# Eleven tables instead of nine by one-hot matmul, two at a time, in a DLRM tower on one core

## The chip, the cores and the metric

One Trainium2 chip, one of its cores. The metric is the time of one execution on the device in microseconds (us); lower is better. Engines: TensorE (PE; its weight loads are PEld), VectorE (DVE), ScalarE (ACT), GpSimd (POOL) and SyncE (SP), which here only issues DMAs.

## The reference

For 512 samples, 26 embedding rows of 128 numbers are looked up, one from each of 26 tables (1000, 1250, 12500 or 125000 rows). With the sample's bottom vector they make 27 features. All 351 dot products of two different features, and the bottom vector, go through three layers. All is float32.

```python
e = jnp.stack([tbl_0[ids[:, 0]], ..., tbl_25[ids[:, 25]]], axis=1)
all_emb = jnp.concatenate([bottom_output[:, None, :], e], axis=1)
gram = jnp.einsum('bfd,bgd->bfg', all_emb, all_emb)
z = gram[:, _TRIU_I, _TRIU_J]
h = jnp.concatenate([z, r_bottom_output], axis=1)
h = jnp.maximum(h @ W_top1 + b_top1, 0.0)
h = jnp.maximum(h @ W_top2 + b_top2, 0.0)
y = h @ W_top3
```

## The kernel before, in words

The samples are four tiles of 128. Features sit in 27 slots: slot 0 is the bottom vector, slots 1 to 9 are the tables that are looked up by matmul (`LOOKED_UP`, nine tables of 1000 rows), slots 10 to 26 the 17 others, gathered row by row.

**Lookup.** A table of 1000 rows lies in SBUF as 125 partitions of 8 rows (`VK`). For each k of the 8, a one-hot matrix of 125 x 512 says which sample wants row 8p + k. TensorE multiplies the table's k-th 125 x 128 slice by it, for all 512 samples at once, and sums over k in PSUM. Precision comes from two terms: the table's value rounded to fp32r (`tab_hi`, cast by ScalarE at line 473) and the rest (`tab_lo`, subtracted by VectorE at line 332); the matmuls are at lines 721 and 725. The one-hots come from `hot`, the table's 512 ids on every partition as int32, minus the partition's first row (line 383). VectorE compares with k (line 388) for 6 or 7 of the 8, ScalarE does the others with a square and a relu (lines 479, 483). A ring of 14 one-hots, a ring of 3 tables and ids, and two split copies of tables tie the engines together by semaphores: the ring places are given back by `s_look`, which TensorE's low matmuls increment. ScalarE copies the found rows from PSUM to `embT` (line 545), the feature matrix with the dimension on partitions, the samples and then the 27 features on the free axis.

**Gathers.** GpSimd issues one indirect DMA of 128 rows for every tile and gathered table (line 313, 68 in all), tile by tile; `emb` has two tiles, so tile 2 waits until the same bank of tile 0 has been transposed. A bank is up to four slots (`BANKS`, five a tile, the last with one slot). TensorE transposes a bank into PSUM (line 612), VectorE (line 329) and ScalarE (line 461) copy banks to `embT` in turn.

**The order after the lookups** is written out by hand, one list for each engine. `gram(t, half)` makes the 27 x 27 products of 64 samples (line 624, two halves a tile). `copy_stage` (line 219) and `copy_products` (line 230) bring them from PSUM to SBUF, split between VectorE and ScalarE; three DMAs move the staged columns to their partitions in `prod` (line 243). `high_products` (line 499) and `low_products` (line 332) split `prod`; layer 1 multiplies the bottom vector's part and the products' part with the split weights (lines 632, 633, 640) into `pH1`; relu (line 522), transpose of h1 (line 676), its split (lines 529, 332), layer 2 (with the bias rows, lines 687, 688) and layer 3 on VectorE (line 372) follow. The weights come in seven chunks of 512 columns into the places of the last tables (line 270) and are split by ScalarE (line 489) and VectorE. Tiles 2 and 3 copy their grams in halves. Before layer 1 of tile 3 TensorE does eight matmuls whose result nobody reads (`stay_busy(WAIT_MOVES)`, line 709).

The DMA queues: SP issues the ids as indices, the tables, `hot` for tables 1 to 8, bottom, b2, w3, the weights and the moves, in program order; ScalarE's queue has `hot` for table 0 alone, GpSimd's the gathers.

Of the kernel before, what the change touches and what calls it, by code (L numbers as in the profile page):

```python
# [21 lines left out]
B = 512  # L22
D = 128
# [13 lines left out]
WAIT_MOVES = 8  # L37
# [4 lines left out]
LOOKED_UP = [3, 4, 5, 7, 8, 10, 20, 24, 25]  # L42
LOOKED = len(LOOKED_UP)
VOCAB = 1000
VP = 125
VP_MAIN = VP // 16 * 16
VK = VOCAB // VP
FIRST_CHUNKS = 2
RING = 3
HOT_RING = 14  # L50
CHUNKS = KTILES + 1 + 2
CHUNK_RING = 2 * RING
# [9 lines left out]
def dve_tiles(i):  # L62

    return VK - 1 - i % 2


def act_tiles_before(i):
    return i * VK - sum(dve_tiles(j) for j in range(i))

# [5 lines left out]
def tower(nc, bottom, ids, hot_ids, tables, w1, w2, b2, w3, out):  # L75
    fp32, fp32r, i32 = mybir.dt.float32, mybir.dt.float32r, mybir.dt.int32
# [3 lines left out]
    with ctx:  # L80
# [10 lines left out]
        hot = sb("hot", [128, RING, B], i32)  # L91

        row0 = sb("row0", [VP, 1], i32)
        row0f = sb("row0f", [VP, 1])
        minus_k = sb("minus_k", [VP, 2])
        tab = sb("tab", [128, RING, VK, D])
        tab_hi = sb("tab_hi", [VP, 2, VK, D], fp32r)
        tab_lo = sb("tab_lo", [VP, 2, VK, D], fp32r)
        square = sb("square", [VP, B])
        onehot = sb("onehot", [VP, HOT_RING, B], fp32r)  # L100
# [9 lines left out]
        w_hi = sb("w_hi", [128, CHUNKS, N1], fp32r)  # L110
        w_lo = sb("w_lo", [128, CHUNKS, N1], fp32r)
# [19 lines left out]
        s_hotids = [sem(f"s_hotids{i}") for i in range(LOOKED)]  # L131
# [9 lines left out]
        s_row0f = sem("s_row0f")  # L141
        s_rel = sem("s_rel")
# [37 lines left out]
        w1_hi, w1_lo = w_hi[:, 0:KTILES + 1, :], w_lo[:, 0:KTILES + 1, :]  # L180
        w2_hi, w2_lo = (w[:, KTILES + 1:, :].rearrange("p c (k n) -> p (c k) n", n=N2) for w in (w_hi, w_lo))
# [10 lines left out]
        def hot_rows(i, k):  # L192
            return onehot[:, (i * VK + k) % HOT_RING, :]

        def wait_hot_free(engine, i, k):

            if i * VK + k >= HOT_RING:
                engine.wait_ge(s_look, i * VK + k - HOT_RING + 1)

        def chunk(c):  # L200

            table = (LOOKED + (c % CHUNK_RING) // 2) % RING
            return tab[:, table, VK // 2 * (c % 2):VK // 2 * (c % 2 + 1), :].rearrange("p k d -> p (k d)")

        def even(t, i):
            return (t * len(BANKS) + i) % 2 == 0
# [40 lines left out]
        def _(sp):  # L247
            def load_table(i, p0, p1, k0, k1, loaded):

                sp.dma_start(tab[p0:p1, i % RING, k0:k1, :], tables[LOOKED_UP[i]].rearrange(  # L250
                    "(p k) d -> p k d", k=VK)[p0:p1, k0:k1, :]).then_inc(loaded, 16)

            def load_lookup(i):
                if i >= RING:
                    sp.wait_ge(s_look, (i - RING + 1) * VK)
                sp.dma_start(hot[:, i % RING, :], hot_ids[i:i + 1, :].broadcast_to([128, B])).then_inc(s_hotids[i], 16)
                load_table(i, 0, VP_MAIN, 0, VK, s_tab[i])
                load_table(i, VP_MAIN, VP, 0, VK, s_tab[i])

            def load_weights(c):  # L260
                if c < CHUNK_RING:
                    sp.wait_ge(s_look, (LOOKED - RING + c // 2 + 1) * VK)
                else:
                    sp.wait_ge(s_wlo, c - CHUNK_RING + 1)
                if c <= KTILES:
                    dst, src = chunk(c), w1[:, c, :]
                else:
                    dst = chunk(c).rearrange("p (k n) -> p k n", n=N2)
                    src = w2.rearrange("(k p) n -> p k n", p=128)[:, 2 * (c - KTILES - 1):2 * (c - KTILES), :]
                sp.dma_start(dst, src).then_inc(s_w[c], 16)  # L270
# [3 lines left out]
            load_table(0, 0, VP_MAIN, 0, VK // 2, s_tab[0])  # L274
            load_table(0, VP_MAIN, VP, 0, VK, s_tab[0])
            load_table(0, 0, VP_MAIN, VK // 2, VK, s_tab0_rest)
            sp.dma_start(bot[:, :, :], bottom.rearrange("(p t) d -> p t d", t=TILES)).then_inc(s_bot, 16)
            load_lookup(1)
            load_lookup(2)
            sp.dma_start(b2s[:, :], b2.unsqueeze(0)).then_inc(s_small, 16)  # L280
            sp.dma_start(w3s[:, :], w3.rearrange("n o -> o n").broadcast_to([128, N2])).then_inc(s_small, 16)
            for i in range(RING, LOOKED):
                load_lookup(i)
# [15 lines left out]
        def _(pool):  # L299
            nc.gpsimd.iota(row0[:, :], [[0, 1]], base=0, channel_multiplier=VK).then_inc(s_row0, 1)  # L300
# [534 lines left out]
```

## Time and profile before

| | us |
|---|---|
| median of 3 runs | 126.18 (125.71 to 126.25) |
| the profiled execution | 124.48 |
| its span, first to last instruction | 122.6 |

Busy in that span: TensorE 90.8, weight loads 73.3, VectorE 77.2, ScalarE 78.4, GpSimd 73.7. The granted clock of TensorE is 0.916 on average. In the rows, the start of an instruction or of a run of equal ones is in us from the span's start; "x8" is a count; what stands after the bar or in brackets is the engine's idle time before it and what ended it. Some matmul records can be missing from a trace.

### The profile page before, as it was taken

The numbers are of one execution on the slowest core, as the hardware profiler recorded it, in microseconds if no ns is written. First come the engines' busy times: TensorE is split into PE (matmuls) and PEld (weight loads), VectorE is DVE, ScalarE is ACT, GpSimd is POOL, SyncE is SP. The second block draws the span as 40 slices with busy tenths as digits, with TensorE's granted clock in tenths as the row PEclk, the third lists the DMA queues.
The fourth block names the chain that finished last, engine by engine and source line by source line (L and its number), as shares of the span: only waits on it lengthen the run. The fifth ranks groups of instructions, "written<-read, shape, count | busy, mean of one in ns | idle before, by whom it ended". The sixth has DMA issues, their size and how long they took to land.

```text
span 122.6 us, 3473 instructions
## 1 busy us (share of the span) xinstructions
PE 90.8 (74%) x1395; PEld 73.3 (60%) x1395; DVE 77.2 (63%) x182; ACT 78.4 (64%) x146; POOL 73.7 (60%) x76
## 2 busy tenths in 40 slices
PE   0005999989989969975318865498998993499992
PEld 0004788858866648854207654396786873488971
DVE  1009999999999996449683158904896328933021
ACT  6214799999999899785405849830899246950130
POOL 3877887788888878888877778787777100100000
PEclk9999999999999999999965799855999999855999
DMA  2789948988988993581222213121221100000000
GB/s 78 211 259 254 241 132 247 235 220 203 222 225 210 242 261 60 204 282 44 68 56 63 55 43 76 43 68 49 52 67 47 43 0 8 8 17 0 0 0 1
DMA packets 7000, 14.08 MB, mean 115 GB/s; under 512 B 2026, under 2 KB 2675, under 8 KB 6984
## 3 DMA queue, kind: packets, MB, share of 16 engines
q1 hardware_dynamic: 4632, 9.11, 27.5%
q0 software_dynamic: 2208, 4.48, 14.8%
q10 hardware_dynamic: 144, 0.26, 0.9%
q8 instruction: 11, 0.18, 0.6%
q14 instruction: 5, 0.04, 0.1%
HBM read 13.71 MB, written 0.00 MB: 112 GB/s over the span
## 4 chain that ended last, share of the span: by engine, by line
POOL 38%; PE 30%; issue 17%; ACT 9%; DMA 3%; DVE 1%; DVEq 0%
POOL emb L313 38%; PE pG L624 7%; PE pH L632 5%; ACT prod L230 5%; PE pH L633 4%; PE pH L640 4%; PE pT L612 2%; PE pG L676 2%; DMA emb<-tbl,idx 2%; PE pT L709 2%; ACT stage L219 2%; DMA idx<-ids 1%; PE pH L687 1%; ACT w_hi L489 1%; PE pH L688 1%
## 5 line engine op out<-in xcount | busy, mean ns | idle before, releaser
L313 POOL DMA_INDIRECT emb<-tbl,idx x68 | 72.4, 1064 | 21.7 <-issue 20.1
L721 PE MATMUL pG<-onehot,tab_hi 125*128 125x512 f32 x72 | 21.0, 431 | 13.0 <-DVE onehot L388 10.6
L721 PEld LDWEIGHTS pG<-onehot,tab_hi 125*128 125x128 f32 x72 | 14.0, 202 | 17.4 <-issue 14.9
L388 DVE TENSOR_SCALAR onehot<-hot 125x512 fp32r<-125x512 int32 x59 | 22.1, 441 | 0.3
L725 PE MATMUL pG<-onehot,tab_lo 125*128 125x512 f32 x72 | 18.0, 391 | 0.0
L624 PE MATMUL pG<-embT 128*26 128x26 f32 x1024 | 13.5, 200 | 5.2 <-issue 4.0
L624 PEld LDWEIGHTS pG<-embT 128*26 128x26 f32 x1024 | 11.6, 112 | 8.5 <-issue 6.2
L612 PE MATMUL pT<-ident,emb 128*128 128x128 f32 x68 | 11.0, 289 | 6.1 <-DMA emb<-tbl,idx 4.7
L725 PEld LDWEIGHTS pG<-onehot,tab_lo 125*128 125x128 f32 x72 | 13.7, 190 | 3.0
L230 ACT COPY prod<-pG 14x64 f32<-14x64 f32 (+7 forms) x48 | 14.7, 306 | 0.6
L230 DVE COPY prod<-pG 14x64 f32<-14x64 f32 (+7 forms) x48 | 14.5, 303 | 0.7
L473 ACT CAST tab_hi<-tab 125x1024 fp32r<-125x1024 f32 (+1 forms) x10 | 9.8, 981 | 5.2 <-DMA tab<-tbl 4.4
L612 PEld LDWEIGHTS pT<-ident,emb 128*128 128x128 f32 x68 | 8.3, 146 | 7.7 <-DMA emb<-tbl,idx 5.0
L219 ACT COPY stage<-pG 10x160 f32<-10x160 f32 (+1 forms) x12 | 6.4, 535 | 9.8 <-PE pG L624 9.6
L329 DVE COPY embT<-pT 128x512 f32<-128x512 f32 (+1 forms) x10 | 6.3, 631 | 9.0 <-PE pT L612 9.0
L479 ACT ACTIVATE square<-hot,minus_k 125x512 f32<-125x512 int32 x13 | 9.4, 725 | 3.5 <-DVE hot L383 3.4
L461 ACT COPY embT<-pT 128x512 f32<-128x512 f32 (+1 forms) x10 | 6.4, 636 | 8.0 <-PE pT L612 8.0
L332 DVE TENSOR_TENSOR tab_lo<-tab,tab_hi 125x1024 fp32r<-125x1024 f32 x9 | 11.0, 1218 | 0.8 <-ACT tab_hi L473 0.7
L545 ACT COPY embT<-pG 128x512 f32<-128x512 f32 x9 | 10.9, 1207 | 0.8 <-PE pG L725 0.8
L383 DVE TENSOR_SCALAR hot<-hot,row0f 125x512 int32<-125x512 int32 x9 | 4.6, 507 | 8.3 <-DMA hot<-hot_ids 8.3
L483 ACT ACTIVATE onehot<-square,ones 125x512 fp32r<-125x512 f32 x13 | 9.4, 724 | 0.4
L219 DVE COPY stage<-pG 10x160 f32<-10x160 f32 (+1 forms) x12 | 6.4, 533 | 3.6 <-PE pG L624 3.4
(69 smaller groups left out, 114.0 us busy)
## 6 DMA issues: line engine op xcount, KB each, us to landing
tab<-tbl SPq DMA_DIRECT2D x8, 448.0 KB
hot<-hot_ids SPq DMA_DIRECT2D x8, 256.0 KB, 4.5
tab<-w SPq DMA_DIRECT2D x7, 256.0 KB, 3.4
emb<-tbl,idx POOLq DMA_INDIRECT x68, 4.4
tab<-tbl SPq DMA_DIRECT2D x9, 52.0 KB
tab<-tbl SPq DMA_DIRECT2D x2, 224.0 KB, 3.8
bot<-bottom SPq DMA_DIRECT2D x1, 256.0 KB, 6.6
hot<-hot_ids ACTq DMA_DIRECT2D x1, 256.0 KB, 6.7
```

What stands on the lines that cost most here:

```text
L219: last = copy(stage[:, :, 64 * halves[0] + s:64 * (halves[-1] + 1):4].rearrange("p k (b i) -> p b i k", i=BANK_GROUPS), gram_blocks(t)[32 ...
L230: last = copy(prod[32 * j:32 * j + rows, :, 64 * halves[0] + s:64 * (halves[-1] + 1):4].rearrange("p k (b i) -> p b i k", i=BANK_GROUPS), ...
L313: nc.gpsimd.indirect_dma_start(out=emb[:, t % 2, g - LOOKED - 1, :], out_offset=None, in_=tables[f], in_offset=bass.IndirectOffsetOnAxis(a ...
L332: return nc.vector.tensor_tensor(lo, whole, hi, ALU.subtract)
L388: nc.vector.tensor_scalar(hot_rows(i, k), hot[0:VP, i % RING, :], float(k), None, ALU.is_equal).then_inc(s_hotv, 1)
L473: nc.scalar.copy(tab_hi[:, i % 2, k:k + step, :], tab[0:VP, i % RING, k:k + step, :]).then_inc(s_tabhi, 1)
L479: nc.scalar.activation(square[:, :], hot[0:VP, i % RING, :], ACT.Square, bias=minus_k[:, k - VK + 2:k - VK + 3]).then_inc(s_sq, 1)
L545: nc.scalar.copy(embT[:, :, :, 1 + i], pG[i % 2][:, 0, :].rearrange("d (t p) -> d t p", p=128)).then_inc(s_lookc, 1)
L612: last = nc.tensor.transpose(bank(t, i)[:, m, :], emb[:, t % 2, g - LOOKED - 1, :], ident[:, :])
L624: last = nc.tensor.matmul(gram_blocks(t)[32 * s:32 * s + ROWS, half, i, :], embT[:, t, p, 0:ROWS], embT[:, t, p, 1:FEATURES], start=True, ...
L721: nc.tensor.matmul(pG[i % 2][:, 0, :], tab_hi[:, i % 2, k, :], hot_rows(i, k), start=(k == 0), stop=False)
L725: nc.tensor.matmul(pG[i % 2][:, 0, :], tab_lo[:, i % 2, k, :], hot_rows(i, k), start=False, stop=(k == VK - 1)).then_inc(s_look, 1)
```

## The change

- `LOOKED_UP` gets two more tables, 2 and 9, of 1250 rows (10 rows a partition). Eleven tables are looked up, 15 are gathered (60 gathers). Banks are four a tile: 4, 4, 4 and 3 slots.
- Table 0 is looked up alone, the others in five pairs (`PAIRS`). A step is one k of a pair: one one-hot instruction for 2 x 512 columns, then four matmuls. The ring holds 8 steps. All one-hots are VectorE's. The comparison is with the row number, which is read per partition, so the subtraction at line 383 goes.
- The ids lie in SBUF for all eleven tables at once, as the low 16 bits (`hot` is int16), loaded in three parts: table 0 by ScalarE's queue, tables 1 and 2, and tables 3 to 10, by SP's, ahead of bottom.
- Tables have four places; high and low parts too, and the split weights lie in the same places afterwards. A table's load waits for the subtraction of the table before it in its place.
- One copy brings both found tables of a pair to `embT`.
- The banks of tiles 0 and 1 are transposed between the pairs (`BANKS_AFTER_PAIR`) and copied by ScalarE alone. In tiles 2 and 3 both engines copy banks in turn, as before.
- In the last tiles the order changes, and `stay_busy` goes.

The diff's core:

```diff
-LOOKED_UP = [3, 4, 5, 7, 8, 10, 20, 24, 25]
+LOOKED_UP = [3, 4, 5, 7, 8, 10, 20, 24, 25, 2, 9]
+VK = [8, 8, 8, 8, 8, 8, 8, 8, 8, 10, 10]
+HOT_RING = 8
+SLOTS = 4
+PAIRS = [range(0, 1)] + [range(i, i + 2) for i in range(1, LOOKED, 2)]
+HOT_PARTS = [range(0, 1), range(1, 3), range(3, LOOKED)]
+BANKS_AFTER_PAIR = {1: [(0, 0)], 2: [(0, 1)], 3: [(0, 2), (0, 3)], 4: [(1, 0), (1, 1)], 5: [(1, 2), (1, 3)]}
...
+        hot = sb("hot", [128, LOOKED, B], i16)
+        tab = sb("tab", [128, SLOTS, VK_MAX, D])
+        high = sb("high", [128, SLOTS, VK_MAX, D], fp32r)
+        low = sb("low", [128, SLOTS, VK_MAX, D], fp32r)
+        onehot = sb("onehot", [VP, HOT_RING, 2, B], fp32r)
...
 SP:
+            def load_whole_table(i):
+                if slot_before(i) >= 0:
+                    sp.wait_ge(s_tablo, slot_before(i) + 1)
...
             load_table(0, 0, VP_MAIN, VK[0] // 2, VK[0], s_tab0_rest)
+            load_hot_ids(1)
+            load_whole_table(1)
+            load_whole_table(2)
+            load_hot_ids(2)
             sp.dma_start(bot[:, :, :], ...)
             b2s, w3s
+            for i in range(3, LOOKED):
+                load_whole_table(i)
...
 VectorE:
+            for n, pair in enumerate(PAIRS):
+                dve.wait_ge(s_hotids[min(n, 2)], 16)
+                following = PAIRS[n + 1] if n + 1 < len(PAIRS) else []
+                for k in range(STEPS[n]):
+                    step = STEPS_BEFORE[n] + k
+                    if step >= HOT_RING:
+                        dve.wait_ge(s_look, step - HOT_RING + 1)
+                    nc.vector.tensor_scalar(hot_rows(n, k), hot[0:VP, pair[0]:pair[-1] + 1, :],
+                                            rowf[VK[pair[0]]][:, k:k + 1], None, ALU.is_equal).then_inc(s_hot, 1)
+                    if n > 0 and k == 3 and following:
+                        low_table(following[0])
+                if n == 0:
+                    low_table(0)
+                    low_table(following[0])
+                if following:
+                    low_table(following[-1])
+            low_weights(0, 4)
...
             copy_stage(0)
             copy_bank(2, 0)
             copy_products(0)
+            low_weights(4, KTILES + 1)
             low_products(0)
...
 ScalarE:
+            for i in range(3):
+                high_table(i)
+            for n in range(len(PAIRS)):
+                copy_found(n)
+                if n + 2 < len(PAIRS):
+                    for i in PAIRS[n + 2]:
+                        high_table(i)
...
+                for t, i in BANKS_AFTER_PAIR.get(n, []):
+                    copy_bank(t, i)
+                if n == len(PAIRS) - 2:
+                    high_weights(0, 4)
+            high_weights(4, CHUNKS)
...
             copy_stage(3, [0])
             copy_products(3, [0])
+            high_h1(2)
             copy_stage(3, [1])
             copy_products(3, [1])
             high_products(3)
...
 TensorE:
+            for n in range(1, len(PAIRS)):
+                pair = PAIRS[n]
+                if n >= 2:
+                    pe.wait_ge(s_lookc, n - 1)
+                pe.wait_ge(s_tablo, pair[-1] + 1)
+                for k in range(STEPS[n]):
+                    pe.wait_ge(s_hot, STEPS_BEFORE[n] + k + 1)
+                    for i in pair:
+                        look(n, i, k, high, k == 0, False)
+                    for i in pair:
+                        last = look(n, i, k, low, False, k == STEPS[n] - 1)
+                    last.then_inc(s_look, 1)
...
+                for t, i in BANKS_AFTER_PAIR[n]:
+                    transpose_bank(t, i)
...
+            pe.wait_ge(s_lookc, len(PAIRS))
             gram(0, 0)
-            transpose_bank(1, 2)
-            transpose_bank(1, 3)
-            transpose_bank(1, 4)
             gram(0, 1)
             transpose_bank(2, 0)
-            transpose_bank(2, 1)
             gram(1, 0)
             layer1_bottom(0)
             gram(1, 1)
+            transpose_bank(2, 1)
             layer1_products(0)
             transpose_bank(2, 2)
             transpose_h1(0)
+            layer2(0)
             transpose_bank(2, 3)
-            layer2(0)
-            transpose_bank(2, 4)
...
             layer2(1)
+            layer1_bottom(2)
+            whole, = h1_parts(2)
+            layer1_high(2, whole, range(0, 2))
             transpose_bank(3, 2)
-            layer1_bottom(2)
-            layer1_products(2)
+            layer1_high(2, whole, range(2, 3))
             transpose_bank(3, 3)
-            transpose_bank(3, 4)
+            layer1_high(2, whole, range(3, 4))
+            layer1_low(2, whole)
+            gram(3, 0)
             transpose_h1(2)
-            gram(3, 0)
             gram(3, 1)
             layer2(2)
             layer1_bottom(3)
-            stay_busy(WAIT_MOVES)
```

## Rows read from the trace of the kernel before

**Rows 1.** Page, part 5: the gathers on GpSimd.
```profile
L313 POOL DMA_INDIRECT emb<-tbl,idx x68 | 72.4, 1064 | 21.7 <-issue 20.1
```

**Rows 2.** Timeline: the joints between the phases (start, length, engine, operation).
```profile
49.44 1.98 PE L725 MATMUL pG<-onehot,tab_lo 125*128 125x512 f32 x8
51.26 1.04 PE L612 MATMUL pT<-ident,emb 128*128 128x128 f32 x8
...
52.69 1.71 PE L624 MATMUL pG<-embT 128*26 128x26 f32 x128 [0.39 <-ACT embT L545]
...
64.41 1.12 PE L612 MATMUL pT<-ident,emb 128*128 128x128 f32 x4 [2.64 <-DMA emb<-tbl,idx]
...
83.86 2.07 PE L624 MATMUL pG<-embT 128*26 128x26 f32 x128 [0.50 <-DVE embT L329]
```

**Rows 3.** Groups by line and form (busy us, mean ns of one, idle before).
```profile
L388 DVE TENSOR_SCALAR onehot<-hot 125x512 fp32r<-125x512 int32 x59 | 22.1, 441 | 0.3
...
L725 PE MATMUL pG<-onehot,tab_lo 125*128 125x512 f32 x72 | 18.0, 391 | 0.0
...
L332 DVE TENSOR_TENSOR tab_lo<-tab,tab_hi 125x1024 fp32r<-125x1024 f32 x9 | 11.0, 1218 | 0.8 <-ACT tab_hi L473 0.7
L545 ACT COPY embT<-pG 128x512 f32<-128x512 f32 x9 | 10.9, 1207 | 0.8 <-PE pG L725 0.8
...
L473 ACT CAST tab_hi<-tab 125x1024 fp32r<-125x1024 f32 x8 | 8.6, 1072 | 2.5 <-DMA tab<-tbl 1.7 <-PE pG L725 0.8
...
L461 ACT COPY embT<-pT 128x512 f32<-128x512 f32 x8 | 5.5, 689 | 7.0 <-PE pT L612 7.0
...
L332 DVE TENSOR_TENSOR w_lo<-tab,w_hi 128x512 fp32r<-128x512 f32 x7 | 4.5, 684 | 2.1 <-ACT w_hi L489 2.1
```

**Rows 4.** Timeline of DVE: the first one-hots.
```profile
9.96 2.58 DVE L388 TENSOR_SCALAR onehot<-hot 125x512 fp32r<-125x512 int32 x7
```

**Rows 5.** Page, part 6: DMA issues (count, KB each, us to landing).
```profile
tab<-tbl SPq DMA_DIRECT2D x8, 448.0 KB
hot<-hot_ids SPq DMA_DIRECT2D x8, 256.0 KB, 4.5
...
tab<-tbl SPq DMA_DIRECT2D x9, 52.0 KB
```

**Rows 6.** Windows from the start (last columns: clock, DMA share, GB/s); ScalarE's wait for table 1.
```profile
0.00:9.00 9.00, 0.00 (x0) 0.00 (x0) 0.34 (x4) 3.13 (x4) 5.71 (x12) 1.00 0.63 182
9.00:14.00 5.00, 3.37 (x8) 2.76 (x9) 4.52 (x10) 2.33 (x3) 3.80 (x4) 1.00 1.04 254
...
13.12 1.04 ACT L473 CAST tab_hi<-tab 125x1024 fp32r<-125x1024 f32 x1 [1.68 <-DMA tab<-tbl]
```

**Rows 7.** Windows with low granted clock (PE, PEld, DVE, ACT, POOL busy; clock, DMA).
```profile
64.40:68.50 4.10, 3.38 (x133) 2.87 (x134) 1.09 (x3) 2.86 (x7) 3.16 (x4) 0.50 0.20 52
...
106.40:113.80 7.40, 6.24 (x25) 5.57 (x25) 3.05 (x11) 2.64 (x9) 0.56 (x1) 0.54 0.03 8
```

**Rows 8.** Stage and product copies of tile 0 in the timeline; the relu's group.
```profile
59.15 1.42 ACT L219 COPY stage<-pG 10x320 f32<-10x320 f32 x2 [1.17 <-PE pG L624]
...
62.41 3.10 DVE L230 COPY prod<-pG 14x128 f32<-14x128 f32 x8
...
L522 ACT ACTIVATE h<-pH 128x256 f32<-128x256 f32 x7 | 2.4, 382 | 9.2 <-PE pH L640 9.2
```

**Rows 9.** Timeline of tile 3: the last high products, and TensorE around the fillers.
```profile
108.90 0.62 ACT L499 CAST prod_hi<-prod 128x512 fp32r<-128x512 f32 x1 [0.40 <-DMA prod<-stage]
...
111.65 0.41 PE L640 MATMUL pT<-w_hi,bot_lo 128*128 128x256 f32 x1
111.86 2.61 PE L709 MATMUL pT<-w_hi 128*128 128x512 f32 x8
114.31 0.28 PE L632 MATMUL pH<-w_hi,prod_hi 128*128 128x256 f32 x1
114.43 0.28 PE L633 MATMUL pH<-w_lo,prod_hi 128*128 128x256 f32 x1
```

More of the change, by code:

```diff
@@ L59, in parts_through, with table_slot, pair_slots, pair_of @@
     return t + 1 + sum(halved <= t for halved in (LAST - 1, LAST))
[L62 to L68, printed above, removed]
+def table_slot(i):
+    return 0 if i == 0 else (i + 1) % SLOTS
+def pair_slots(pair):
+    return slice(table_slot(pair[0]), table_slot(pair[0]) + len(pair))
+def pair_of(i):
+    return (i + 1) // 2
+def slot_before(i):
+    return {3: 0}.get(i, i - SLOTS)
 BANKS = [range(g, min(g + 4, FEATURES)) for g in range(LOOKED + 1, FEATURES, 4)]
-def tower(nc, bottom, ids, hot_ids, tables, w1, w2, b2, w3, out):
-    fp32, fp32r, i32 = mybir.dt.float32, mybir.dt.float32r, mybir.dt.int32
+def tower(nc, bottom, ids, hot_ids, tables, w1_in, w2_in, b2, w3, out):
+    fp32, fp32r, i32, i16 = mybir.dt.float32, mybir.dt.float32r, mybir.dt.int32, mybir.dt.int16
     ALU, ACT = mybir.AluOpType, mybir.ActivationFunctionType
@@ L190, in bank, with hot_rows, found, on_dve @@
                 "d (f p) -> d f p", p=128)
[L192 to L206, printed above, removed]
+        def hot_rows(n, k):
+            return onehot[:, (STEPS_BEFORE[n] + k) % HOT_RING, 0:len(PAIRS[n]), :]
+        def found(n):
+            return pG[n % 2][:, 0:len(PAIRS[n]), :]
+        def on_dve(t, i):
+            return t >= TILES_EARLY and (t * len(BANKS) + i) % 2 == 0
+        def copied_through(t, i):
+            places = [(u, j) for u in range(TILES) for j in range(len(BANKS))]
+            through = places[:t * len(BANKS) + i + 1]
+            return sum(on_dve(*p) for p in through), sum(not on_dve(*p) for p in through)
         def gram_blocks(t):
@@ L488, in high_weights @@
                     act.wait_ge(s_w[c], 16)
-                    nc.scalar.copy(w_hi[:, c, :], chunk(c)).then_inc(s_whi, 1)
+                    act.wait_ge(s_look, STEPS_BEFORE[pair_of(table_under(c)) + 1])
+                    nc.scalar.copy(w1(high, c), chunk(c)).then_inc(s_whi, 1)
             def high_products(t):
@@ L694, in layer2_low @@
                 tiles = slice(2 * half, 2 * half + 2)
-                last = low_terms(pH2[:, :], h1T_lo[:, tiles, :], w2_hi[:, tiles, :], half == 1,
+                last = low_terms(pH2[:, :], h1T_lo[:, tiles, :], [w2(high, k) for k in (2 * half, 2 * half + 1)], half == 1,
                                  lambda k: pe.wait_ge(s_h1lo, 2 * t + half + 1))
@@ new lines, in _ @@
+            for k in range(STEPS[0]):
+                pe.wait_ge(s_tabhi, 1 if k < STEPS[0] // 2 else 2)
+                pe.wait_ge(s_hot, k + 1)
+                look(0, 0, k, high, k == 0, False)
+            pe.wait_ge(s_tablo, 1)
+            for k in range(STEPS[0]):
+                look(0, 0, k, low, False, k == STEPS[0] - 1).then_inc(s_look, 1)
+            for n in range(1, len(PAIRS)):
+                pair = PAIRS[n]
+                if n >= 2:
[8 more added lines that the diff above has]
+                    last.then_inc(s_look, 1)
+                if n == 1:
```

287 lines of the change are left out of this document (102 added, 185 removed).

## The prediction

> **What bounds the kernel now.** I read the groups by line, then the timeline at the joints between the phases, then windows for DMA and clock. The kernel has two halves. In the first, VectorE, ScalarE and TensorE share the lookups of nine tables, 4.7 us a table; the last lookup leaves TensorE at 51.4 [rows 2]. Beside it GpSimd gathers all the time, 68 gathers at (72.4 + 20.1) / 68 = 1.36 us each [rows 1]. In the second half TensorE first meets gathers that have not landed: the grams of tile 1 stand behind a transpose that starts at 64.4 after 2.64 us of waiting for a gather. The first gram of tile 2 starts at 83.9, and the end comes 38.7 us later [rows 2]. Gathers and lookups pull against each other, and the change trades one for the other: 8 gathers less (about 11 us of GpSimd), 20 table tiles more (92 for 72).
>
> **The lookup half, priced.** *One-hots.* Before, 59 on VectorE and 13 on ScalarE; after, all on VectorE: 8 of 512 columns, 42 of 1024. Subtractions take 1218 ns for 1024 elements and 684 for 512, so 1.04 ns an element. A one-hot of 512 takes 441, less than 512 x 1.04 = 534: it goes two elements at a time. Seven in a row take 2.58, or 0.37 each [rows 3, 4]; 512 more columns add 0.27: 0.64. The per-partition scalar may add a little: 0.65. No row has 16-bit input with 32-bit output. Bounds: 0.60 and, one element at a time, 0.10 + 1024 x 1.04 = 1.17. I take 0.65, since the nearest row is the same operation with 32-bit ids.
>
> The Trainium skill (VectorE: DVE Perf Modes, "What auto-detection actually checks") wants one SBUF source, an SBUF destination and even outer dimensions for the two-port mode, and all tensors 16-bit for four at a time. By it the sum stays as it is, and the halves bring VectorE nothing; no row here shows such a mix.
>
> *TensorE.* Eight matmuls take 1.98 with the last at 0.391, so one starts every 0.227 us [rows 2, 3]. A step of a pair (two tables, high and low) has four: 0.91. Per pair that is 7.3 plus 0.55 for each bank transposed (eight transposes take 1.04 [rows 2]). VectorE has 8 x 0.65 + 2 x 1.22 = 7.6 a pair and may run eight steps ahead, so from pair 2 on TensorE is the slightly longer engine. ScalarE, freed of 26 activations, has two casts (1.07), a copy of the found rows and one or two bank copies (0.69) [rows 3]: at most 6 us a pair. That cover is thin in one place: the cast for the next pair but one stands behind the copy of the found rows, and VectorE wants it after its step 3.
>
> *The copy of found rows.* Single elements at a pitch of 27 cost 1.21 for 512; runs of four adjacent ones 0.69 [rows 3]. A pair writes runs of two, 1024 elements: between 1.1 (the cast's rate) and 2.4 (twice the single). I take 1.2, the single's price for 512 runs. At 2.4 each pair loses up to 0.9.
>
> The Trainium skill (SBUF — State Buffer, the note on "cachelines" under "Door 1: The DMA port swizzle") says that two hits in a 16-byte line are enough for full bandwidth; by that the copy would cost 1.1, and the sum would hardly move.
>
> *The first tables.* This step I expect to decide. VectorE's order is written out: after step 3 of pair 1 it subtracts table 3, and steps 4 to 7 are queued behind; TensorE waits for them, GpSimd does not. Table 3's load stands on SP's queue behind the ids' second block of eight rows, 128 x 8 x 1 KB = 1024 KB, and behind bottom (256) and w3 (128); before, 256 KB of ids went with each table of 448 + 52 KB [rows 5]. Up to and with table 3: ids 52 as indices, 128, 256 and 1024 as halves; four tables of 500; 256; 128: 3,844 KB or 3.94 MB. The queues moved 9 x 182 = 1.64 MB in the first 9 us, then 254 GB/s while full [rows 6]. With ten gathers of 64 KB among it, 4.6 MB are reached at 9 + 2.96 / 0.254 = 20.7. How late a landing shows: table 1 ended ScalarE's wait at 13.12, when 2.68 MB had moved, of which 1.86 of its own queue up to it and 0.3 of gathers [rows 6]; the remaining 0.5 are 2 us. So table 3 lands at 22.6 (20.5 with 285 GB/s and 1 us; 23.5 at worst). Then cast 1.07, subtraction 1.22, one-hot 0.65 and hops: step 4 is ready at 25.7.
>
> Pair 1 itself starts at 16.8: the first ids have half the bytes and the subtraction of the row number goes (first one-hot at about 9.0 for 9.96 [rows 4]), pair 0 takes 3.3, three subtractions 3.7, a one-hot 0.65. Four steps end at 20.4, TensorE stands 5.3 us, the last four steps take 3.6 and end at 29.3. What the start gains is swallowed here. The idle costs clock too: after an idle before 64.4 TensorE was granted 0.50, its 1.2 GHz level, until 68.5 [rows 7]. I add 0.9 (0 to 2): pair 1 ends at 30.2. From there three pairs of 32 matmuls (21.8), one of 40 (9.1), transposes of bottom and six banks (3.6): **the lookups end at 64.7**, 13.3 later than before, but with tile 1 transposed (its last two banks 1 us on). GpSimd is no limit: at 1.36 us gather 45 (the last of tile 2) is out by 66 and gather 60 by 85.
>
> **Up to the first gram of tile 2.** Each piece waits for the one before. Copy of found rows 1.3; grams of tile 0 at 1.7 each [rows 2], 3.4; stage copies 1.4; then on VectorE bank 0.7, products 3.1 and the subtraction of weight chunk 4, 0.7 [rows 3, 8], which now stands behind the products and for which layer 1 of tile 0 waits: 10.6, with TensorE idle for 3 of it, so at its low clock again. Bottom part 1.1; second gram of tile 1 1.9; stage 1.5; bank 0.7; products 3.1; relu, transpose and high half 0.4 each [rows 8]; layer 2 2.2; last bank and its copy 1.1; hops 0.6: **24.0**. Before it was 83.9 - 51.4 = 32.5. So that gram stands at 88.7, 4.8 later than before.
>
> **The last tiles.** Before, the last high products were ready at 108.90 + 0.62 = 109.5, and TensorE was busy with layer 2 of tile 2, the bottom parts and eight filler matmuls (2.61, to 114.1) before layer 1 [rows 9]: 4.6 us. After, tile 3's gram stands ahead of the transpose of h1(2), but ScalarE and VectorE now do h1(2) before the second stage copy, so the last high products come at the old offset. Layer 2 is out of the way and no filler stands there: gain 4.4. But the filler held the clock. Without it idles of 1 to 2 us stand right before layer 1, and from 106.4 to 113.8 the clock was already 0.54 [rows 7]; 38 small matmuls cost 0.21 there and 0.12 at 2.4 GHz [rows 9], 3.4 in all. I give back 1.5. **Net 2.9** (1.0 to 4.4). The smaller banks of tiles 2 and 3 hide beside ScalarE's products and count nothing; uncovered they are 0.3.
>
> **Sum.** 64.7 + 24.0 + 38.7 - 2.9 = 124.5 against a span of 122.6: +1.9. The profiled execution took 124.48, the runs' median is 126.18; the same 1.9 on the median gives 128.0.
>
> **Rivals.** *A, the forecast:* table 3 late by about 5 us. Own range 125.6 to 130.5.
> *B, faster:* table 3 is there in time, because full queues with rows of 4 and 8 KB move more than 254 GB/s and a landing shows at once. It decides from a landing below 18: pair 1 runs through to 24.1, the lookups end at 58.6, the span is 118.4, the time 121.9. Each microsecond of landing in between gives one. Against it: 3.9 MB and the gathers in 15 us want nearly 300 GB/s.
> *C, slower:* with 16-bit ids VectorE goes one element at a time. A step costs 1.17, a pair 11.8, VectorE bounds the phase from its start, the lookups end near 79, and the time is near 143. For it, only that no row shows the mix; against it, that the 32-bit form goes two at a time.
> *D, slower:* TensorE stays at 1.2 GHz through tile 3's layers: 1.9 more, 130.
> *E, a draw:* half the stall and the whole gain at the end: 124.5 to 126.8. Here the change only swaps gather waits for a longer lookup half.
>
> **Numbers.** A 0.45, B 0.30, C 0.07, D 0.08, E 0.10. A measurement of this kernel can tell about 0.5% from no change, here 125.6 to 126.8. Slower: 0.39 of A, C, D: 0.54. Same: 0.06 of A and of E: 0.12. Faster: B and 0.04 of E: 0.34. The range, 122.5 to 132, leaves out C and the ends of B and D, under 0.2.
>
> **What would show it.** Right: an idle of VectorE of 3 to 6 us before the subtraction of table 3, ended by a cast that a table's load released near 22 to 24; a one-hot of 1024 near 0.7; TensorE idle about 5 us near 20 to 26; the last lookup near 64 to 65; no wait of TensorE for a gather; layer 1 of tile 3 right behind the last high products. Wrong: a cast of table 3 before 19 is B; a one-hot over 1 us is C; from the lookups' end to the first gram of tile 2 not 22 to 26, the middle sum failed; from there to the end not 34 to 38, that of the last tiles.

## The result, and the profile after

| | before | after |
|---|---|---|
| median, us (lowest to highest, runs) | 125.94 (124.27 to 126.25, 4) | 136.3 (134.27 to 138.18, 4) |
| the profiled execution, its span | 124.48, 122.6 | 136.68, 134.9 |
| granted clock of TensorE, mean | 0.916 | 0.924 |

The ratio is 1.081, 95% interval 1.042 to 1.120: slower, as forecast, but by 10.4 us for a forecast of 1.9, and outside the range. Ratios are taken from the fast runs of both kernels, medians from all runs. The span is 134.9 where the sum had 124.5, so 10.4 us are to be found in its terms (that the two differences are equal is chance: one is from median to median, the other from sum to span).

The page of the kernel after, from parts 1 and 2 (busy time; tenths of a slice of 3.4 us; the granted clock):

```profile
PE 99.4 (74%) x1419; PEld 79.8 (59%) x1419; DVE 82.9 (61%) x159; ACT 62.7 (46%) x121; POOL 67.3 (50%) x69
...
PE   0009983393499999989997851797987999736992
...
DVE  1029770993984089799995049479469742883212
...
PEclk9999999859959999999999999559999999995599
```

TensorE has two holes in the lookup half, slices 7 to 8 and 10 to 11, and the clock falls behind each of them (the 8 and 5, and the next 5, in the third row). Later there are two more low stretches. The groups that answer to [rows 1, 3] (busy us, mean ns of one, idle before):

```profile
L340 POOL DMA_INDIRECT emb<-tbl,idx x60 | 65.9, 1098 | 19.3 <-issue 17.7
...
L420 DVE TENSOR_SCALAR onehot<-hot,rowf 125x1024 fp32r<-125x1024 int16 x42 | 29.3, 755 | 0.7 <-PE pG L719 0.7
...
L498 ACT COPY embT<-pG 128x1024 f32<-128x1024 f32 x5 | 7.1, 1429 | 26.3 <-PE pG L719 26.3
```

The one-hot of 1024 costs 755 ns alone, and four in a row take 2.74, so 0.69 each for a forecast 0.65. That is 0.67 ns an element, below the 1.04 of the subtractions, so the halves go two elements at a time, as the 32-bit ids did. The copy of found rows costs 1.43 for a forecast 1.2. By the Trainium skill's note on cachelines (SBUF — State Buffer, "Door 1: The DMA port swizzle"), two hits in a 16-byte line are enough, and the copy would cost an estimated 1.1. The trace is 0.33 above that; but at a pitch of 27 elements one pair in four lies across the edge of such a line, and no run here tells whether these pairs are the cost.

The waits of the kernel after (us in total, times, longest):

```profile
PE pG L719 <- DVE onehot L420: 15.5, 5, 9.9
ACT high L491 <- DMA tab<-tbl: 15.2, 6, 4.5
DVE low L359 <- ACT high L491: 13.1, 5, 5.2
...
PE pT L619 <- ACT embT L560: 4.0, 1, 4.0
```

No wait of TensorE for a gather is left. The first three rows are totals over the whole run (the 9.9 is the wait for the first one-hot of all); the stall that was forecast is one wait in each of them, of 4.25, 4.54 and 4.37. The fourth row was not in the forecast. The timeline of both, from table 3 to pair 2:

```profile
23.75 1.23 DVE L359 TENSOR_TENSOR low<-tab,high 125x1024 fp32r<-125x1024 f32 x1 [4.37 <-ACT high L491]
...
25.70 0.75 PE L719 MATMUL pG<-onehot,high 125*128 125x512 f32 x2 [4.25 <-DVE onehot L420]
...
31.06 0.60 PE L745 MATMUL pT<-ident,bot 128*128 128x128 f32 x4
31.26 1.39 ACT L498 COPY embT<-pG 128x1024 f32<-128x1024 f32 x1 [5.30 <-PE pG L719]
...
32.50 1.99 ACT L491 CAST high<-tab 125x1024 fp32r<-125x1024 f32 x2
...
34.39 1.18 ACT L560 COPY embT<-pT 128x512 f32<-128x512 f32 x1
...
35.71 0.63 PE L619 MATMUL pT<-ident,emb 128*128 128x128 f32 x4 [4.05 <-ACT embT L560]
```

Step 4 of pair 1 starts at 25.70, the forecast's 25.7 to the tenth. Then pair 1 ends, TensorE transposes bottom, and stands 4.05 us at the first bank of tile 0. `transpose_bank` waits there for `s_banka >= 1`, which is ScalarE's copy of bottom (line 560). On ScalarE that copy is queued behind the copy of the found rows and two casts. Pair 2 is queued behind the bank on TensorE. The wait guards nothing: bottom was transposed into `pT[1]`, this bank goes to `pT[0]`.

Windows of the kernel after (PE, PEld, DVE, ACT, POOL busy; clock, DMA share, GB/s) show what the two stands cost in clock:

```profile
25.70:31.00 5.30, 5.30 (x16) 4.19 (x17) 5.30 (x8) 0.27 (x1) 4.08 (x5) 0.68 1.01 229
...
28.00:29.00 1.00, 1.00 (x4) 0.81 (x3) 1.00 (x2) 0.00 (x0) 0.69 (x2) 0.50 1.09 205
...
30.00:31.00 1.00, 1.00 (x6) 0.81 (x5) 1.00 (x3) 0.00 (x0) 1.00 (x1) 1.00 1.01 238
...
31.70:35.70 4.00, 0.00 (x0) 0.02 (x1) 2.12 (x3) 3.87 (x4) 3.31 (x3) 1.00 0.57 144
36.00:39.30 3.30, 3.30 (x13) 2.57 (x11) 3.30 (x5) 0.68 (x1) 2.69 (x3) 0.58 0.79 234
...
86.90:91.00 4.10, 4.10 (x137) 3.76 (x137) 2.34 (x4) 2.29 (x4) 0.00 (x0) 0.50 0.07 20
120.50:128.60 8.10, 7.02 (x37) 6.73 (x37) 2.73 (x9) 2.25 (x7) 0.28 (x1) 0.58 0.03 6
```

After the two stands the granted clock was 0.68 and 0.58 on average, though TensorE was busy without a gap. Cut finer, these means are the two levels one after the other: behind the first stand 0.50 (1.2 GHz) from 27.0 to 29.0 and 1.00 (2.4 GHz) from 30.0 on, behind the second 0.50 from 37.0 to 39.0 and 1.00 from 40.0 on. The last 16 matmuls of pair 1 took 5.36 us for 3.6, pair 2 9.0 us for the 7.3 of a pair at 2.4 GHz. The grams after the lookups and the last layer 1:

```profile
78.97 0.25 PE L632 MATMUL pG<-embT 128*26 128x26 f32 x6 [1.47 <-issue]
...
83.06 0.29 PE L632 MATMUL pG<-embT 128*26 128x26 f32 x11 [1.87 <-issue]
...
85.30 0.80 PE L640 MATMUL pH<-high,bot_hi 128*128 128x512 f32 x1 [1.94 <-DVE low L359]
...
98.28 1.26 PE L632 MATMUL pG<-embT 128*26 128x26 f32 x128 [0.72 <-ACT embT L478]
...
124.02 0.62 ACT L515 CAST prod_hi<-prod 128x512 fp32r<-128x512 f32 x1 [2.22 <-DMA prod<-stage]
124.69 0.58 PE L640 MATMUL pH<-high,prod_hi 128*128 128x256 f32 x1 [1.08 <-ACT prod_hi L515]
```

The lookups end at 72.1 (forecast 64.7: +7.4), 26.2 us later stands the first gram of tile 2 (24.0: +2.2), and 36.6 us later the end (35.8: +0.8).

### The profile page after: what moved, and what is told of

Read it like the earlier page. It is cut to its first block, busy times and chain, and to the rows that moved or that the text cites. A ratio compares the mean times of both kernels' runs of the same rounds, so it can differ in the third digit from the quotient of the medians.

```text
span 134.9 us, 3380 instructions
## 1 busy us (share of the span) xinstructions
PE 99.4 (74%) x1419; PEld 79.8 (59%) x1419; DVE 82.9 (61%) x159; ACT 62.7 (46%) x121; POOL 67.3 (50%) x69
## 4 chain that ended last, share of the span: by engine, by line
PE 49%; ACT 15%; DMA 14%; DVE 12%; issue 8%; SPq 0%; ACTq 0%; POOLq 0%; DVEq 0%
PE pG L719 23%; PE pG L632 7%; DMA tab<-tbl 6%; PE pH L640 5%; DMA hot<-hot_ids 5%; DVE onehot L420 4%; ACT high L491 4%; DVE low L359 4%; PE pH L641 4%; PE pH L647 4%; ACT prod L252 3%; DMA prod<-stage 3%; PE pT L619 3%; DVE prod L252 2%; ACT stage L241 2%
## 5 line engine op out<-in xcount | busy, mean ns | idle before, releaser
L719 PE MATMUL pG<-onehot,high 125*128 125x512 f32 x92 | 32.2, 441 | 15.5 <-DVE onehot L420 15.5
L420 DVE TENSOR_SCALAR onehot<-hot,rowf 125x1024 fp32r<-125x1024 int16 (+1 forms) x50 | 32.6, 711 | 8.6 <-DMA hot<-hot_ids 7.9
L719 PEld LDWEIGHTS pG<-onehot,high 125*128 125x128 f32 x92 | 18.6, 209 | 21.1 <-issue 9.9
L719 PE MATMUL pG<-onehot,low 125*128 125x512 f32 x92 | 30.9, 426 | 0.1
L359 DVE TENSOR_TENSOR low<-tab,high 125x1024 fp32r<-125x1024 f32 (+2 forms) x18 | 18.3, 1039 | 13.1 <-ACT high L491 13.1
L719 PEld LDWEIGHTS pG<-onehot,low 125*128 125x128 f32 x92 | 19.1, 209 | 5.2 <-DVE low L359 0.8
L498 ACT COPY embT<-pG 128x1024 f32<-128x1024 f32 (+1 forms) x6 | 8.4, 1392 | 27.8 <-PE pG L719 27.8
L491 ACT CAST high<-tab 125x1024 fp32r<-125x1024 f32 (+2 forms) x12 | 11.8, 1014 | 15.2 <-DMA tab<-tbl 15.2
L640 PE MATMUL pH<-high,prod_hi 128*128 128x512 f32 (+1 forms) x16 | 7.4, 465 | 1.1 <-ACT prod_hi L515 1.1
L641 PE MATMUL pH<-low,prod_hi 128*128 128x512 f32 (+1 forms) x16 | 6.8, 426 | 0.0
```

Source lines behind the costliest of these rows:

```text
L359: return nc.vector.tensor_tensor(lo, whole, hi, ALU.subtract)
L420: nc.vector.tensor_scalar(hot_rows(n, k), hot[0:VP, pair[0]:pair[-1] + 1, :], rowf[VK[pair[0]]][:, k:k + 1], None, ALU.is_equal).then_inc( ...
L491: nc.scalar.copy(high[0:VP, table_slot(i), k:k + step, :], tab[0:VP, table_slot(i), k:k + step, :]).then_inc(s_tabhi, 1)
L498: nc.scalar.copy(embT[:, :, :, 1 + pair[0]:2 + pair[-1]].rearrange("d t p f -> d (t p) f"), found(n).rearrange("d f b -> d b f")).then_inc ...
L640: nc.tensor.matmul(psum, a_hi[:, k, :], b_hi[k], start=start and k == 0, stop=False)
L641: nc.tensor.matmul(psum, a_hi[:, k, :], b_lo[k], start=False, stop=False)
```

## The experiments

Each batch ran beside the kernel before on the same chip. Its medians were 124.53 (runs 1 to 4), 124.61 (12 to 14) and 124.12 (15 to 17) in the three batches whose times are read, and 125.94 beside the changed kernel, which was not run again in any of them. So a time set against its 136.3 can be off by the 1.8 us between these medians, and across batches only differences over 2 us are read.

**1. One wait away.** The first bank no longer waits for the bottom copy; the second still does.

```diff
                 if n < 0:
-                    pe.wait_ge(s_banka, 1)
+                    if i == 1:
+                        pe.wait_ge(s_banka, 1)
```

> Changed kernel; TensorE's transpose of tile 0's first bank no longer waits for the copy of the bottom vector, which uses the other PSUM bank. Theory (the two stalls of TensorE in the first pairs are what the prediction missed or only half counted): the 4.05 us of idle at 31.7 to 35.7 goes, and with it most of the half-clock stretch behind it (1.7 us): pair 2 ends near 39.5 instead of 45.1, the time falls by 4.5 to 6 us. Rival (VectorE's subtraction of table 5, held back by the casts behind the copy of found rows, is the real bound of pair 2): steps 4 to 7 of pair 2 still start after 35.4, and the time falls by less than 2.5 us.

130.2 us (129.18 to 130.46), ratio 1.058 (1.043 to 1.074), span 128.2. In its timeline:

```profile
31.35 0.60 PE L746 MATMUL pT<-ident,bot 128*128 128x128 f32 x4
31.55 1.43 ACT L498 COPY embT<-pG 128x1024 f32<-128x1024 f32 x1 [6.07 <-PE pG L720]
31.79 0.60 PE L620 MATMUL pT<-ident,emb 128*128 128x128 f32 x4
...
34.71 1.22 ACT L560 COPY embT<-pT 128x512 f32<-128x512 f32 x1
```

The bank now stands 2.9 us ahead of the bottom copy. The lookups end at 66.6, 5.5 sooner, and the time is 6.1 less by the medians, 4.7 less if each is counted from the kernel before in its own batch. The one wait that the forecast left out, with the clock behind it, is the larger half of the miss.

**2. Table 3 earlier.** Its load goes ahead of the ids of tables 3 to 10.

```diff
             load_whole_table(2)
+            load_whole_table(3)
             load_hot_ids(2)
...
-            for i in range(3, LOOKED):
+            for i in range(4, LOOKED):
```

> Changed kernel; the load of table 3 is issued ahead of the big block of ids, bottom, b2 and w3. Theory: table 3 lands near 18 instead of 22.7, VectorE's idle of 4.4 us before its subtraction and TensorE's of 4.25 us go, pair 1 ends near 25 to 26 and no clock is lost there: 4.5 to 6 us less. Rival (the ids for pair 2 or bottom are then the late ones, the stall only moves): the ids land near 24 to 26, TensorE stands before pair 2 instead, and the time falls by less than 2 us.

135.85 us (133.92 to 137.09). Table 3 was cast at 17.62, five us sooner, and nothing was gained:

```profile
17.62 1.05 ACT L492 CAST high<-tab 125x1024 fp32r<-125x1024 f32 x1 [1.01 <-DMA tab<-tbl]
...
27.23 1.04 ACT L492 CAST high<-tab 125x1024 fp32r<-125x1024 f32 x1 [8.56 <-DMA tab<-tbl]
...
28.31 1.23 DVE L360 TENSOR_TENSOR low<-tab,high 125x1024 fp32r<-125x1024 f32 x1 [5.72 <-ACT high L492]
...
35.04 1.08 PE L620 MATMUL pT<-ident,emb 128*128 128x128 f32 x4 [10.01 <-ACT embT L561]
```

Now table 4 is behind the 1 MB of ids, VectorE stands 5.72 at its subtraction, and TensorE, done with pair 1, stands 10 us for the bottom copy. The rival held. But the edit does more than change an order. Table 3 goes to the place of table 0 (`slot_before(3)` is 0), so its load waits for the subtraction of table 0, and SP, which issues in program order, holds back all that stands behind it:

```profile
13.27 0.76 SPq L272 DMA_DIRECT2D tab<-tbl  x2
...
14.07 0.35 SPq L283 DMA_DIRECT2D hot<-hot_ids  x1
```

The ids go out at 14.07, in the changed kernel at 5.53, and from 12 to 14 the queues ran half empty (107 GB/s at a DMA share of 0.44, for 254 at 1.02 in the changed kernel). How much of table 4's delay is the block's size and how much this wait of SP, no run takes apart.

**3. Weight chunk 4 earlier.** VectorE subtracts chunks 4 to 6 ahead of the stage copy of tile 0.

```diff
+            low_weights(4, CHUNKS)
             copy_stage(0)
             copy_bank(2, 0)
             copy_products(0)
-            low_weights(4, KTILES + 1)
             low_products(0)
             copy_stage(1)
-            low_weights(KTILES + 1, CHUNKS)
```

> Changed kernel; VectorE subtracts weight chunks 4 to 6 before the first stage copy, where it stands idle for 6.6 us, not behind the products of tiles 0 and 1. Theory: TensorE's wait of 1.9 us for chunk 4 goes, and 2 us of VectorE's work leave the chain from the lookups to the first gram of tile 2: that distance falls from 26.2 to about 24, the time by 1.5 to 2.5 us. Rival (ScalarE's products set the pace there in any case): less than 0.7 us.

133.56 us (131.2 to 135.75), which overlaps with the 134.27 to 138.18 of the changed kernel. The wait at layer 1 of tile 0 was gone, but from the last lookup to the first gram of tile 2 it still took 26.1 us, with TensorE's "issue" waits of 1.70 and 1.25 in it and a granted clock of 0.55 to 0.60 from 82 to 90. Inconclusive by itself. The other runs tell more: with the same edit the distance was 24.8, 24.4, 24.8 and 24.8 us (runs 4, 12, 13, 17), without it 26.2, 26.6, 26.1 and 26.6 (the changed kernel, runs 1, 2, 16) and 28.8 (run 15). So the early chunk is worth about 2 us there, as the theory had it.

**4. All three.**

> The three edits together. Theory: the stalls are separate and add: lookups end near 61 instead of 72.1, the first gram of tile 2 starts near 85, the time is 122 to 125, level with the kernel before. Rival (the lookup phase is then bound by the chain copy of found rows, cast, subtraction, one-hot of each pair): lookups end at 64 or later and the time stays above 127.

128.32 us (127.96 to 131.68), ratio 1.043 (1.025 to 1.062). Table 4 was cast at 27.10 after 8.46 us of waiting for its load, and TensorE stood 4.79 us before 30.21. The lookups ended at 66.2. The rival's numbers came true, but not its reason: the phase was held up by table 4's landing, not by the chain from copy to one-hot. As in run 2, 1 MB of ids stood in one piece ahead of table 4, and SP held the ids back until 14.13; moving table 3 alone only chose which table was late.

**5 to 11. Ids split, fillers, moves, in two batches whose times can't be read.** The split kernel has edits 1 and 3, and loads the ids of tables 3 and 4 apart from the rest:

```diff
-HOT_PARTS = [range(0, 1), range(1, 3), range(3, LOOKED)]
+HOT_PARTS = [range(0, 1), range(1, 3), range(3, 5), range(5, LOOKED)]
...
             load_hot_ids(2)
             sp.dma_start(bot[:, :, :], ...)
+            load_whole_table(3)
+            load_whole_table(4)
+            load_hot_ids(3)
...
-            for i in range(3, LOOKED):
+            for i in range(5, LOOKED):
```

> The e4 kernel, but the big block of ids is split: the two rows of pair 2 come before bottom, tables 3 and 4 follow, and the six other rows come behind table 4. In e4 table 3 was in time and table 4 was the late one (cast at 27.1), with VectorE idle for 5.6 us. Theory (what stands in the queue ahead of what pair 1 and 2 need is the cost, whichever piece it is): tables 3 and 4 are cast by 18 and 22, pair 1 ends near 24.5, lookups end at 60 to 61.5, the time is 122.5 to 124. Rival (the total of bytes in the first 25 us bounds, so a third piece is late, bottom or table 5): lookups end at 64 or later, the time falls by less than 2 us against e4's 128.3.

The kernel before without its fillers:

```diff
-            stay_busy(WAIT_MOVES)
```

> The kernel before, without its eight filler matmuls ahead of layer 1 of tile 3. This does the one part of the change alone. The prediction's working (the filler stood 2.6 us on the path, the clock gives 1.3 of it back): 0.5 to 2 us less than before. Rival (the filler is what brings the clock up for all of tile 3's layers): no change or up to 1.5 us more, with TensorE at 1.2 GHz through layer 1 and 2 of tile 3.

The split kernel with eight fillers ahead of layer 1 of tile 3:

```diff
             layer1_bottom(3)
+            for _ in range(8):
+                nc.tensor.matmul(pT[0][:, :], w1(high, 0)[:, 0:128], w1(high, 0), start=True, stop=True)
```

> The e5 kernel with eight fillers put back ahead of layer 1 of tile 3. There TensorE is done with the bottom parts only about 1.1 us before the high products are ready. Theory: the fillers cost more than the idle they fill: layer 1 starts 2 us later, half of it returned by the clock: 1 to 1.5 us slower than e5. Rival (the clock is raised in time): same or up to 1 us faster.

The split kernel with GpSimd's one move on SP's queue:

```diff
-                for step in MOVES if t < LAST else MOVES[1:]:
+                for step in MOVES:
...
-            move(nc.gpsimd, s_movedp, *MOVES[0])
```

> The e5 kernel with all three moves of tile 3 on SP's queue, none on GpSimd's. In all runs of the changed kernel GpSimd's move took 2.8 to 3.7 us to land, 1.9 in the kernel before, and ScalarE's last cast waited 1.3 to 2.2 us for the moves. Theory (GpSimd's DMA is late after its long idle): the wait of the last cast falls to 0.8 to 1.2 us, the time by 0.5 to 1 us. Rival (the landing of any move takes so long there): one more issue of 0.7 us in SP's row makes it 0 to 0.7 us slower.

In this batch and in its repeat (e8_split, e9_nofill, e10_fill, e11_spmove) every kernel ran far slower, before too (171.21 and 171.69 us), so only the order within a batch says anything. The longest waits of the kernel before without fillers had no work behind them:

```profile
PEld pG L721 <- issue: 37.3, 11, 9.5
PEld pG L624 <- issue: 25.2, 33, 2.5
...
DVE onehot L388 <- remote: 20.4, 6, 9.9
```

Split 150.6 and 151.06; with fillers 151.25 and 152.19; with the move on SP 149.72 and 150.25; before without fillers 167.72 and 166.1 (160.38 to 173.07). The differences from the split kernel lie within the spread of its runs. None of the expectations in us can be judged by them. Experiments 12 to 14 ask for the split, the move and the kernel before without fillers again; fillers in the split kernel were not run again, so what they cost there stays open.

**12. The split, again.**

> Bank transposes no longer held by the bottom copy, weights of chunk 4 earlier, and the ids of tables 3 to 10 in two loads (tables 3 and 4 ahead of bottom, tables 5 to 10 behind table 4). Theory (the late load of table 3, moved to table 4 by the other order, is the second cause of the long lookup half): table 3 cast near 19, table 4 near 21, TensorE idle under 1 us between 20 and 35, pair 1 ends near 26, lookups end at 60 to 62, so 4 to 6 us less than with the bank wait alone removed (130.2): 124 to 126. Rival (pairs 2 to 5 take up the gain, since later tables or the copies of found rows now come last): lookups end at 64 or later, 128 or more.

122.49 us (121.5 to 123.39) beside 124.61 (123.63 to 125.73); ratio 0.983 (0.976 to 0.989), span 120.9: 1.1 to 2.4% faster than the kernel before, and 13.8 us below the changed kernel's median. In its timeline:

```profile
18.10 1.06 ACT L493 CAST high<-tab 125x1024 fp32r<-125x1024 f32 x1 [0.72 <-DMA tab<-tbl]
...
21.55 1.05 ACT L493 CAST high<-tab 125x1024 fp32r<-125x1024 f32 x1 [2.40 <-DMA tab<-tbl]
...
25.14 1.46 ACT L500 COPY embT<-pG 128x1024 f32<-128x1024 f32 x1 [2.53 <-PE pG L722]
...
61.89 0.93 PE L622 MATMUL pT<-ident,emb 128*128 128x128 f32 x7
```

Its windows (columns as above) from pair 1's end to the grams of tile 3:

```profile
25.00:35.00 10.00, 8.59 (x43) 6.88 (x42) 7.95 (x11) 5.20 (x5) 7.87 (x8) 1.00 1.04 238
35.00:62.00 27.00, 26.31 (x124) 21.25 (x123) 25.74 (x36) 14.30 (x17) 20.90 (x21) 1.00 0.59 155
62.00:86.30 24.30, 16.52 (x568) 12.89 (x567) 14.17 (x30) 16.24 (x34) 18.04 (x19) 1.00 0.23 58
86.30:107.00 20.70, 17.81 (x580) 14.69 (x581) 13.45 (x41) 13.63 (x42) 0.00 (x0) 1.00 0.03 7
```

Pair 1 ends near 25 and the lookups at 61.9, ten us sooner than in the changed kernel. The clock stays at 2.4 GHz up to 107. The theory held for the casts, pair 1 and the end of the lookups, but for one stand of 1.4 us near 30; the time came 1.5 us below its range. Against run 4 the split changes two things at once: the block is smaller, and SP's wait for table 0's subtraction (table 3 issued at 14.02) now holds back only the ids of tables 5 to 10 and what follows.

**13. The move on SP, again.**

> As the split kernel, with the one move of tile 3 that GpSimd issued put on SP's queue. Theory (GpSimd's move lands 1 to 2 us later than one of SP after a long idle): 0.5 to 1.5 us less than the split kernel, and layer 1 of tile 3 starts that much sooner. Rival (the three moves in one queue follow each other and end no sooner): equal within 0.4.

122.82 us (121.96 to 123.33) in the same batch. From the first issue to the high products it took 3.85 us (SP issued from 108.52, the cast stood at 112.37), with GpSimd 3.03 (108.37 to 111.40). The rival held: GpSimd's late landing is no loss that SP would save.

**14. The kernel before without fillers, again.**

> The kernel before without its eight filler matmuls ahead of layer 1 of tile 3. My sum gave the removal 4.4 us less 1.5 for the clock, in the changed kernel. Theory (the fillers cost what they stand on the path, less the clock): 1 to 3 us less than before, 123 to 125. Rival (without them the clock falls for layers 1 and 2 of tile 3 and takes it back): within 0.6 of before.

122.94 us (122.34 to 123.77), ratio 0.989 (0.983 to 0.995). In its timeline the products start 1.66 us sooner than in [rows 9]:

```profile
112.44 0.41 PE L640 MATMUL pT<-w_hi,bot_lo 128*128 128x256 f32 x1
112.65 0.41 PE L632 MATMUL pH<-w_hi,prod_hi 128*128 128x256 f32 x1
```

From there to the end it is 9.35 us for 8.3 with the fillers. So layer 1 started 1.66 us sooner and took 1.05 back in clock, which leaves the 0.6 by which the profiled spans differ; the medians differ by 1.67. The 1.66 is not the fillers alone: they stood for 2.45 us in [rows 9] (111.86 to 114.31), but in this run the bottom parts ended 0.8 us later, behind an "issue" wait of 2.62 us where the kernel before had 1.97. The theory held by the medians; the share of each part stays uncertain by about a us.

**15. The split without the other cures.**

> The changed kernel with nothing but the ids of tables 3 to 10 in two loads (tables 3 and 4 ahead of bottom); the bank transposes still wait for the bottom copy. Theory (two waits in a row: curing the first lengthens the second, since the bottom copy stands behind the casts of tables 5 and 6, which came at 28.0 and 30.7 when the split was in): pair 1 ends near 25, TensorE then stands 7 to 8 us until about 33, the lookups end at 67 to 70, 130 to 134. Rival (the waits add up, so that each cure gives what it is worth alone: 136.3 less the 7 to 8 us between the changed kernel without the bank wait and the split version): 127 to 129.

133.47 us (132.55 to 136.44), ratio 1.088 (1.064 to 1.112). The rows are from the execution of 136.44 us, so they may stand a us or two late. Its timeline:

```profile
26.62 1.41 ACT L501 COPY embT<-pG 128x1024 f32<-128x1024 f32 x1 [4.15 <-PE pG L722]
...
30.42 1.05 ACT L494 CAST high<-tab 125x1024 fp32r<-125x1024 f32 x1 [1.50 <-DMA tab<-tbl]
31.37 1.17 ACT L563 COPY embT<-pT 128x512 f32<-128x512 f32 x1
...
32.69 1.09 PE L622 MATMUL pT<-ident,emb 128*128 128x128 f32 x4 [5.67 <-ACT embT L563]
```

Pair 1 is through near 26.6, but TensorE stands 5.67 us (for 7 to 8 expected, and 4.05 in the changed kernel), pair 2 still starts after 32.7, and the lookups end at 69.9. The waits don't add up: a cure of the first lengthens the second. Alone, the bank's wait was worth 6.1 and the split 2.8; together (run 16) 12.2 of the changed kernel's 136.3, across batches. Counted from the kernel before in each batch it is 4.7, 1.0 and 10.4: the sizes differ, and together is more than the sum both ways.

**16. Split and bank wait, chunk 4 left late.**

> The split ids and the bank transposes freed of the bottom copy, without the earlier split of weight chunk 4. Theory (the subtraction of chunk 4 behind the products of tile 0 holds layer 1 of tile 0 for about 2 us, and half of it shows): 123.5 to 125, against 122.5 with it. Rival (the wait is hidden, other waits take its place): within 0.4 of 122.5.

124.12 us (123.39 to 126.49), ratio 1.012 (0.995 to 1.030), span 121.6 for 120.9 with the early chunk. The sign is that of the theory, and the 1.6 us between the medians are within what batches differ by. The traces are clearer: from the last lookup to the first gram of tile 2 it took 26.6 us for 24.4 in run 12, with 2.20 of waiting for chunk 4 in it. The spans differ by 0.7 only, because here the lookups ended at 60.4, 1.5 sooner than in run 12.

**17. Ids pair by pair.** `HOT_PARTS = PAIRS`, the last two parts ahead of tables 7 and 9.

> As the split version, but the ids are loaded pair by pair, each ahead of its tables, instead of 768 KB in one load ahead of table 5. Theory (there table 5 was late by 1.4 us, VectorE stood 2.1 and TensorE 1.4 to 1.8 near 30): the stand of TensorE near 30 goes, the lookups end 1 to 2 us sooner, near 60.3, 121 to 122. Rival (table 6 or 7 comes late in its place): within 0.5 of 122.5.

122.42 us (121.13 to 125.25), span 120.2; ratio 0.997 (0.974 to 1.019). The lookups ended at 60.5, as in the theory, but the time is the rival's. The stand near 30 was gone, but so it was in run 16, where the ids had not been divided further: when table 5 lands varies. The version is not shown to be better than run 12's.

## Why the prediction was wrong

*What bounds the phases: right.* The first half became the bound, gathers ceased to matter, the sign follows. It doesn't hang on the wait that was overlooked: with that wait gone, run 1 is still 5.8% slower than the kernel before.

*The first tables: right.* Cast of table 3 at 22.68 (22.6), step 4 at 25.70 (25.7). Pair 1 ended at 31.06 (30.2); the low clock behind the stand cost 1.7, more than the 0.9 allowed. The forecast of the landing left one thing out without harm: table 3's load waits for its place and went out at 13.70. The queues were still full then (a DMA share of 1.02 from 12 to 14), so the bytes ahead decided, as the sum had it; with the ids split, in run 15, the same load took 6.6 us from issue to cast for 9.0 here.

*The failed step* is the sentence behind it: "From there three pairs of 32 matmuls (21.8), one of 40 (9.1), transposes of bottom and six banks (3.6)". It priced the transposes by their own length and put pair 2 right behind pair 1. The bank's semaphore wait for ScalarE was not followed to what ScalarE had queued ahead. The text had said of ScalarE that its "cover is thin in one place", and looked only at the cast. Measured in its place: 4.05 of waiting, 1.7 of clock in pair 2, 0.9 at pair 1 and 0.8 in small waits, 7.4 in sum. Run 1 shows the first two: 5.5 of them went with one wait.

*Rival B (121.9, "table 3 is there in time")* was priced as if one condition decided it. Run 2 meets that condition, with table 3 cast at 17.62, and gives 135.85, since table 4 then came late. Run 15 nearly meets it, with table 3 cast at 19.30 and table 4 at 21.41, and gives 133.47. With the bank's wait gone as well (runs 12 and 16) the time is 122.5 to 124.1, near B's. Two conditions had to hold, so 0.30 looks too much for it, and the range lacked the case in which both waits stand.

*Up to the first gram of tile 2: undersized by 2.2.* The two grams of tile 0 were priced at 1.7 each from the row of one; with "issue" waits of 1.47 in the second they took 5.4. The wait for chunk 4 was foreseen.

*The last tiles: right in size.* 36.6 for 35.8. Counted from the first gram of tile 2, layer 1 of tile 3 stood 4.0 us sooner than before (26.4 for 30.4; forecast 4.4), and from there to the end it took 10.2 for 8.3, so 1.9 were given back where I had 1.5. Rival D, with 1.9 more than that, 3.4 in all, did not come: the clock was 0.50 from 122 to 128 and 1.00 again from 129 on. In run 14, on the kernel before, 1.05 were given back.

*One-hots: right,* and rival C did not come: 0.69 for 0.65. By the Trainium skill (VectorE: DVE Perf Modes, "What auto-detection actually checks") such a mix goes two at a time, and the trace agrees.

## What to carry to other kernels

A wait that is moved to a new place waits for whatever its releaser has queued ahead there: for every semaphore that a moved instruction waits on, read the releasing engine's list up to that release, also where the moved instruction itself costs half a microsecond. A transfer of 1 MB in one piece on a queue is a bar for all behind it: order and cut loads by when each part is wanted. The same holds for a load that must wait for its place: whatever stands behind it in the issuing engine's program goes out later too, so moving one table past the block only made the next one late. Two waits in a row hide each other; take both away before judging either.

## What the runs showed of the hardware

- After each stand of 4 us TensorE ran back to back, and its granted clock was 0.50 for 2 to 3 us of that work (27.0 to 29.0, 37.0 to 39.0), then 1.00, with no pause between. In run 12 the longest stands of that phase were under 2 us, and no window up to 107 shows less than 1.00. The second stall cost about 1.4 times its length, (4.05 + 1.7) / 4.05.
- The fall of the clock is not tied to the lookups: in windows of 4 and 8 us where TensorE was busy for all or most of the time it was 0.50 and 0.58, both behind idles of 1.9 to 2.2 us. The length of one such idle does not decide it: in run 15 TensorE stood 2.08 us before 17.50 and was granted 0.50 from 18 to 20, in run 12 it stood 2.08 us before 82.50, in a window at 1.00.
- In stretches of hundreds of short matmuls TensorE stood 0.9 to 2.2 us at a time with "issue", that is, for nothing the profile shows (1.47, 1.87, 2.17 in the changed kernel; 1.65, 1.05, 1.00, 1.31, 0.88, 1.89 in run 12). They come at nearly the same matmul each time: the 251st of tile 0's grams in both, and in runs 1 to 4, 13 and 15 to 17 too. No run here took their cause apart.
- In two batches all kernels took 22 to 38% longer, with waits of up to 9.9 us on TensorE and VectorE for no work of the kernel. The split kernel was slowed less than before (150.6 for 171.2, where it is 122.5 for 124.6 else).
